# A language-model tower on one core: semaphores raised by TensorE, token numbers loaded in 8 KB runs, values formed ahead of scores

## The reference

```python
def tok(input_seq, emb_W, emb_b, Wq, bq, Wk, bk, Wv, bv, Wo, bo):
    emb = emb_W.T[input_seq] + emb_b
    q = (emb @ Wq.T + bq); k = (emb @ Wk.T + bk); v = (emb @ Wv.T + bv)   # 16 heads of 16
    probs = softmax(einsum('bqhd,bkhd->bhqk', q, k) / sqrt(d))
    y = einsum('bhqk,bkhd->bqhd', probs, v).reshape(b, s, e) @ Wo.T + bo + emb
    return layernorm over a sequence of y
h = tok(x, ...)
h = h + attn(layernorm(h), ...)
h = h + ffn(layernorm(h), ...)     # the 32 x 128 x 256 f32 result
```

## Time and profile before

| | us |
|---|---|
| median of 3 runs | 889.64 (888.16 to 892.07) |
| span of the profiled execution, first to last instruction | 888.7 |
| TensorE busy in the span | 710.7 |
| VectorE busy | 617.1 |
| GpSimd busy | 452.7 |
| ScalarE busy | 355.4 |

### The profile page before, as it was taken

One profiled execution on the slowest core, in us unless ns is written; L12 is line 12 of the kernel. 1 busy time (PEld: TensorE's weight loads), 2 busy tenths in 40 slices (PEclk: granted clock), 3 DMA queues, 4 the chain that ended last, 5 costly groups with the idle time before them and its releaser, 6 DMA issues. The chain is left out here.

```text
span 888.7 us, 20544 instructions
## 1 busy us (share of the span) xinstructions
PE 710.7 (80%) x7708; PEld 478.2 (54%) x7708; DVE 617.1 (69%) x913; ACT 355.4 (40%) x561; POOL 452.7 (51%) x257
## 2 busy tenths in 40 slices
PE   3576759886999999999999999976899689875744
PEld 3354534444677777777777777755676323322221
DVE  3599947888999999999999999963676501100005
ACT  2366635353445545445455544433555211010100
POOL 1588700002999999999999999981111000000000
PEclk9799869998999999999999999987999879979765
DMA  5100000000001010000000000005800679999936
GB/s 109 48 1 0 0 1 0 0 0 14 8 14 38 13 35 12 11 7 12 12 12 12 12 12 8 12 14 198 313 25 1 233 271 412 417 416 416 418 135 213
DMA packets 48891, 86.34 MB, mean 97 GB/s; under 512 B 5232, under 2 KB 32432, under 8 KB 48848
## 3 DMA queue, kind: packets, MB, share of 16 engines
q1 hardware_dynamic: 43248, 81.23, 25.1%
q10 hardware_dynamic: 5600, 4.53, 1.6%
HBM read 76.31 MB, written 9.44 MB: 96 GB/s over the span
## 5 line engine op out<-in xcount | busy, mean ns | idle before, releaser
L898 POOL TENSOR_TENSOR read<-state,q_pos 128x1024 f32<-128x1024 f32 x128 | 300.2, 2365 | 28.5 <-DVE state L1007 22.4
L1007 DVE TENSOR_TENSOR_SCAN state<-fac,ps_up 128x1024 f32<-128x1024 f32 x128 | 290.1, 2278 | 8.6 <-ACT fac L942 8.2
L942 ACT ACTIVATE fac<-ps_xf 128x1016 f32<-128x1016 f32 x128 | 130.2, 1018 | 176.1 <-PE ps_xf L1041 160.2
L1041 PE MATMUL ps_xf<-hot,xtab 64*128 64x128 f32 x2048 | 148.4, 284 | 11.0 <-ACT fac L942 8.9
L1041 PEld LDWEIGHTS ps_xf<-hot,xtab 64*128 64x128 f32 x2048 | 125.4, 188 | 58.0 <-ACT fac L942 43.4
L1041 PE MATMUL ps_up<-hot,utab 64*128 64x128 f32 x2048 | 140.0, 276 | 19.3 <-DVE state L1007 19.3
L1041 PEld LDWEIGHTS ps_up<-hot,utab 64*128 64x128 f32 x2048 | 126.4, 189 | 24.9 <-issue 17.6
L907 POOL TENSOR_TENSOR utab<-tab 128x1024 f32 (+1 forms) x32 | 64.7, 2022 | 94.4 <-SPq L85 94.4
L1086 PE MATMUL ps_o<-read,sel 128*32 128x256 f32 x1024 | 82.4, 393 | 4.0 <-POOL read L898 4.0
L1627 DVE COPY h_t<-ps_ht 128x512 f32<-128x512 f32 x16 | 10.3, 686 | 75.7 <-PE ps_ht L1655 75.7
L997 DVE TENSOR_TENSOR xtab<-tab,ps_k 128x1024 f32<-128x1024 f32 x64 | 59.5, 930 | 1.5 <-PE ps_k L1033 1.5
(11 more groups left out here) (202 smaller groups left out, 995.0 us busy)
## 6 DMA issues: line engine op xcount, KB each, us to landing
w_sb<-in_L_ffn_w SPq DMA_DIRECT2D x32, 2048.0 KB, 19.4
rec_out<-osb SPq DMA_DIRECT2D x128, 32.0 KB, 1.5
ao<-rec_out SPq DMA_DIRECT2D x8, 512.0 KB, 4.4
out_dram<-res ACTq DMA_DIRECT2D x8, 512.0 KB, 2.8
tok<-in_x SPq DMA_DIRECT2D x2, 512.0 KB, 11.2
exp_out<-eo SPq DMA_DIRECT2D x8, 128.0 KB
oq<-exp_out SPq DMA_DIRECT2D x2, 512.0 KB, 3.9
w_nat<-in_L_tok_Wq SPq DMA_DIRECT2D x1, 256.0 KB, 3.1
```

What stands on the lines that cost most here:

```text
L898: nc.gpsimd.tensor_tensor(read[n % 2][:], state[n % 4][:].rearrange("p (b i t) -> p b i t", b=2, i=IB), q_pos[x.s][:, :, x.k].unsqueeze(2) ...
L942: nc.scalar.activation(fac[n % 2][:].rearrange("p (n t) -> p n t", t=T)[:, :, 1:], ps_x[:].rearrange("p (n t) -> p n t", t=T)[:, :, 1:], A ...
L1007: nc.vector.tensor_tensor_scan(state[n % 4][:], fac[n % 2][:], ps_u[n % 2][:], 0.0, ALU.mult, ALU.add)\
L1041: last = nc.tensor.matmul(dst[:, b * 512 + col * T:b * 512 + (col + 1) * T], stationary[rows], pos[rows], start=True, stop=True)
```

## The change

The first block's semaphores are raised by TensorE, as the first thing in its program, and SP no longer does it. The token numbers become SP's first loads. They are paired b and b + 16, so each half of `tok` is one run of 2,048 numbers (8 KB) of x, which each of the 64 partitions gets whole. `emb_bc` and `bqk` move from ScalarE's queue to SP's, behind the token numbers, and Wv and Wo stay on SP behind those. Wq and Wk move to ScalarE's queue, behind `emb_w`. TensorE waits for the identity alone (`id_ok`) before its first transposes, and waits for `masks` just ahead of line 346. Wv is transposed together with Wq and Wk, ahead of q and k, and ScalarE copies it ahead of the logarithm. TensorE forms values and transposed embedding ahead of the scores. At the end of the kernel a quad now holds two sequences of the first half of the batch and two of the second, so its store becomes two DMAs of 256 KB, and `f_out` counts 32 per quad.

```diff
--- before.py
+++ after.py
@@ -192,32 +192,32 @@
         block = ctx.enter_context(nc.Block())
         ld_w = [sem(f"ld_w{n}") for n in range(4)]
         ld_e, ld_bq, ld_bv, ld_x = (sem(n) for n in ("ld_e", "ld_bq", "ld_bv", "ld_x"))
-        masks, w_tp, w_cp = sem("masks"), sem("w_tp"), sem("w_cp")
+        id_ok, masks, w_tp, w_cp = sem("id_ok"), sem("masks"), sem("w_tp"), sem("w_cp")
         emb_ok, q_mm, q_ok, k_ok = (sem(n) for n in ("emb_ok", "q_mm", "q_ok", "k_ok"))
         s_mm, e_tp, c_dg, c_mm, c1_ok, ln_ok = (sem(n) for n in ("s_mm", "e_tp", "c_dg", "c_mm", "c1_ok", "ln_ok"))
         vch = sem("v_chain0")
 
+        def weights(eng, n):
+            w = ("L0_tok_Wq", "L0_tok_Wk", "L0_tok_Wv", "L0_tok_Wo")[n]
+            eng.dma_start(w_nat[:, n], a[w].rearrange("(k p) i -> p k i", p=P)).then_inc(ld_w[n], 16)
+
         @block.sync
         def _(sp):
-            def weights(n):
-                w = ("L0_tok_Wq", "L0_tok_Wk", "L0_tok_Wv", "L0_tok_Wo")[n]
-                sp.dma_start(w_nat[:, n], a[w].rearrange("(k p) i -> p k i", p=P)).then_inc(ld_w[n], 16)
-
-            for n in range(2):
-                weights(n)
             for s in range(2):
-                src = a["x"].rearrange("(r s) t -> s r t", s=2)[s]
-                sp.dma_start(tok[s * C:(s + 1) * C], src.partition_broadcast(C)).then_inc(ld_x, 16)
+                src = a["x"].rearrange("(s r) t -> s (r t)", s=2)[s]
+                sp.dma_start(tok[s * C:(s + 1) * C].rearrange("p r t -> p (r t)"), src.partition_broadcast(C))\
+                    .then_inc(ld_x, 16)
+            sp.dma_start(emb_bc[:], a["L0_tok_emb_b"].rearrange("(k p) -> p k", p=P), allow_slow_non_contiguous=True).then_inc(ld_e, 16)
+            sp.dma_start(bqk[:, 0], a["L0_tok_bq"].rearrange("(k p) -> p k", p=P), allow_slow_non_contiguous=True).then_inc(ld_bq, 16)
+            sp.dma_start(bqk[:, 1], a["L0_tok_bk"].rearrange("(k p) -> p k", p=P), allow_slow_non_contiguous=True).then_inc(ld_bq, 16)
             for n in range(2, 4):
-                weights(n)
-            m["start"](sp)
+                weights(sp, n)
 
         @block.scalar
         def _(act):
             act.dma_start(emb_w[:], a["L0_tok_emb_W"].rearrange("(k p) c -> p k c", p=P)).then_inc(ld_e, 16)
-            act.dma_start(emb_bc[:], a["L0_tok_emb_b"].rearrange("(k p) -> p k", p=P), allow_slow_non_contiguous=True).then_inc(ld_e, 16)
-            act.dma_start(bqk[:, 0], a["L0_tok_bq"].rearrange("(k p) -> p k", p=P), allow_slow_non_contiguous=True).then_inc(ld_bq, 16)
-            act.dma_start(bqk[:, 1], a["L0_tok_bk"].rearrange("(k p) -> p k", p=P), allow_slow_non_contiguous=True).then_inc(ld_bq, 16)
+            for n in range(2):
+                weights(act, n)
             act.dma_start(bv_b[:], bcast_rows(a["L0_tok_bv"])).then_inc(ld_bv, 16)
             act.dma_start(bo_b[:], bcast_rows(a["L0_tok_bo"])).then_inc(ld_bv, 16)
             nc.scalar.preload_act_table(ACT.Ln)
@@ -226,12 +226,11 @@
                 act.wait_ge(w_tp, START + n + 1)
                 nc.scalar.copy(w_t[:, n], ps[n][:].rearrange("p (k o) -> p k o", k=KT)).then_inc(w_cp, 1)
 
-            for n in range(2):
+            for n in range(3):
                 copy_weights(n)
             act.wait_ge(c1_ok, START + 1)
             nc.scalar.activation(cnt1[:], cnt1[:], ACT.Ln).then_inc(ln_ok, 1)
-            for n in range(2, 4):
-                copy_weights(n)
+            copy_weights(3)
             act.wait_ge(ln_ok, START + 1)
             nc.scalar.preload_act_table(ACT.Exp)
 
@@ -248,8 +247,8 @@
             pch = Chain(pool, sem("p_chain0"))
 
             pch.link(nc.gpsimd.memset(ident[:], 0.0))
-            pch.link(nc.gpsimd.affine_select(out=ident[:], in_=ident[:], compare_op=ALU.not_equal, fill=1.0,
-                                             base=0, pattern=[[-1, P]], channel_multiplier=1))
+            nc.gpsimd.affine_select(out=ident[:], in_=ident[:], compare_op=ALU.not_equal, fill=1.0, base=0,
+                                    pattern=[[-1, P]], channel_multiplier=1).then_inc(id_ok, 1)
             for s in range(2):
                 pch.link(nc.gpsimd.iota(cid[s * C:(s + 1) * C], pattern=[[0, 1]], base=0, channel_multiplier=1,
                                         allow_small_or_imprecise_dtypes=True))
@@ -267,6 +266,7 @@
             pch.link(nc.gpsimd.memset(same_half[:], 0.0))
             for s in range(2):
                 pch.link(nc.gpsimd.memset(same_half[s * C:(s + 1) * C, s * C:(s + 1) * C], 1.0))
+            pool.wait_ge(id_ok, START + 1)
             nc.gpsimd.tensor_tensor(ident64[:], ident[:, 0:C], ident[:, C:P], ALU.add).then_inc(masks, 1)
             pch.link(nc.gpsimd.memset(m["sel"][:], 0.0))
             for q in range(4):
@@ -324,8 +324,9 @@
                                                    w_nat[:, n, ko, ki * P:(ki + 1) * P], ident[:])
                 last.then_inc(w_tp, 1)
 
-            pe.wait_ge(masks, START + 1)
-            for n in range(2):
+            m["start"](pe)
+            pe.wait_ge(id_ok, START + 1)
+            for n in range(3):
                 transpose_weights(n)
             pe.wait_ge(emb_ok, START + 1)
             pe.wait_ge(w_cp, START + 2)
@@ -339,24 +340,24 @@
                                             w_t[:, 1, ki, ko * P:(ko + 1) * P], emb_t[:, ki, 0:C],
                                             start=ki == 0, stop=ki == KT - 1)
             last.then_inc(q_mm, 1)
-            for n in range(2, 4):
-                transpose_weights(n)
+            transpose_weights(3)
             pe.wait_ge(c_dg, START + 1)
+            pe.wait_ge(masks, START + 1)
             for k in range(2):
                 nc.tensor.matmul(ps[6 + k][:], same_half[:],
                                  log_diag[:, k * PAIRS // 2:(k + 1) * PAIRS // 2].rearrange("p r c -> p (r c)"),
                                  start=True, stop=True).then_inc(c_mm, 1)
-            pe.wait_ge(q_ok, START + 1)
-            for k in range(KT):
-                pe.wait_ge(k_ok, START + k + 1)
-                nc.tensor.matmul(ps[k][:], q_t[:, k], k_heads[:, k].rearrange("p h c -> p (h c)"),
-                                 start=True, stop=True).then_inc(s_mm, 1)
             pe.wait_ge(w_cp, START + 3)
             for ki in range(KT):
                 nc.tensor.matmul(ps[5][:, 0:E], emb_t[:, ki], w_t[:, 2, ki], start=ki == 0, stop=ki == KT - 1)
             for k in range(KT):
                 last = nc.tensor.transpose(ps[5][:, E + k * P:E + (k + 1) * P], emb_t[:, k], ident[:])
             last.then_inc(e_tp, 1)
+            pe.wait_ge(q_ok, START + 1)
+            for k in range(KT):
+                pe.wait_ge(k_ok, START + k + 1)
+                nc.tensor.matmul(ps[k][:], q_t[:, k], k_heads[:, k].rearrange("p h c -> p (h c)"),
+                                 start=True, stop=True).then_inc(s_mm, 1)
 
 
     with ExitStack() as ctx:
@@ -1732,23 +1733,23 @@
             with nc.vector.Fori(0, TURNS) as i:
                 for s in range(2):
                     dve.wait_ge(f_mm[s], START + i + 1)
-                    dve.wait_ge(f_out[s], START + 16 * i)
+                    dve.wait_ge(f_out[s], START + 32 * i)
                     for j in range(QB):
-                        at = 2 * (j % 2) + j // 2
-                        last = nc.vector.tensor_tensor(res[s][:, at:at + 1], psx[s][j][:, 0:E].unsqueeze(1),
+                        last = nc.vector.tensor_tensor(res[s][:, j:j + 1], psx[s][j][:, 0:E].unsqueeze(1),
                                                        h2[:, bass.ds(2 * QB * i + QB * s + j, 1)], ALU.add)
                     last.then_inc(f_add[s], 1)
 
         @block.scalar
         def _(act):
-            dst = out.rearrange("(q j) t e -> q t j e", j=QB)
+            dst = out.rearrange("(z q p) t e -> z q t p e", z=2, p=2)
             with nc.scalar.Fori(0, TURNS) as i:
                 for s in range(2):
                     act.wait_ge(f_add[s], START + i + 1)
-                    act.dma_start(dst[bass.ds(2 * i + s, 1)].rearrange("q t j e -> (q t) j e"), res[s][:])\
-                        .then_inc(f_out[s], 16)
+                    for z in range(2):
+                        act.dma_start(dst[z, bass.ds(2 * i + s, 1)].rearrange("q t p e -> (q t) p e"),
+                                      res[s][:, 2 * z:2 * z + 2]).then_inc(f_out[s], 16)
             for s in range(2):
-                act.wait_ge(f_out[s], START + 16 * TURNS)
+                act.wait_ge(f_out[s], START + 32 * TURNS)
 
 
 # ---- launch: one core; inputs and outputs as the reference has them ----
```

## The result

| | before | changed | predicted |
|---|---|---|---|
| median of 5 runs, us | 889.35 (887.8 to 892.07) | 883.46 (881.69 to 884.7) | 881.9 (878.2 to 886.2) |
| ratio | | 0.9927, 95% interval 0.9908 to 0.9945 | 0.991 |
| span of the profiled execution, us | 888.7 | 880.2 | 881.0 |
| line 433 (now 434) begins, us | 29.69 | 23.18 | 21.7 |
| first store of the result to the end, us | 18.5 | 18.4 | 18.8 |

What follows compares the result with a forecast made beforehand. The first block was taken as bound by the token load, VectorE's counting, TensorE's last three steps and VectorE's tail. 8.0 us saved there less 0.3 for stores gave 7.7: 889.64 to 881.9 us, range 878.2 to 886.2.

Steps and rivals of the forecast that it cites:

- Semaphores: First block's start: TensorE raises all 22 in 1.5 us, through at 2.3 us, beside the loads.
- Token load: First block: 1.05 MB at 231 GB/s takes 4.5 us, landing at 7.1; `onehot` begins at 8.1 instead of 15.57.
- Weights: First block, two queues: Wv lands at 9.0, Wo's transposes end at 14.7, so line 346 begins then instead of 21.24.
- The clock: TensorE's line 346 runs partly at the upper clock level: 2.5 us, between 1.71 and 3.37.
- Values first: First block's end: values 1.25 us, then scores to ScalarE's last copy 2.50; block ends at 20.9 instead of 28.9.
- Stores: Result stores at the kernel's end, split in two: a cost of 0.3 us, at most 1.7, no gain.
- The sum: Whole kernel: 8.0 us from the first block less 0.3 for stores, 7.7 us, median 881.9.
- The loads are no faster: Rival on the token load: 8 KB runs no quicker than 512-byte ones; gain 2.2 us, 887.4; chance 0.08.
- The lower clock throughout: Rival: TensorE stays at the lower clock in the first block; gain 4.5 less 0.3, 885.4; chance 0.10.
- later block took the gain back: Rival: attention over classes meets a lower clock for longer, some 6 us, result within 0.5%; chance 0.03.
- the stores did not become the bound: Denies the rival that split stores bound the kernel, adding say 12 us, 894; chance 0.05.

Runs made afterwards that it cites:

- the run with the halves on two queues: The changed kernel with the second half of the token numbers as ScalarE's first load, the first half on SP; median 883.4 us, ratio 0.9924.
- the run with short runs first: The changed kernel with token numbers still first on SP's queue, but in the old 512-byte runs and one store per quad; median 886.55 us, ratio 0.9961.
- the small loads last: Token halves on two queues and bias on ScalarE's queue, with the two bqk loads moved behind Wv and Wo; median 884.9 us, ratio 0.9928.
- Long runs alone: The kernel before with only the new pairing: 8 KB token runs in the old queue place, stores in two; median 887.71 us, ratio 0.997.
- the run with the filled gap: The kernel before with 8 KB runs and stores in two, plus ten unused TensorE transposes behind Wo's; line 436 began at 27.32 us.

## Why the prediction was right

**Semaphores.** Right. They were priced at nothing. In the two runs on them TensorE's raising was worth 0.1 us with the old loads and -0.2 with the new ones.

**Token load.** The direction was right, and this is the term that was mis-sized. Forecast: 1 MB at 231 GB/s, there at 7.1. Measured: the second half at 9.9. The 231 GB/s itself was good (128 packets of 612 ns on 16 engines are 4.9 us). But I added it up as if Wq, Wk and the embedding beside it took no time from the same engines. From 2 to 8 us the rate was 88 to 370 GB/s for everything together, and the token packets ran from 2.2 to 9.2 us. In the run with the halves on two queues, where Wq and Wk stand behind a half, they ran from 2.2 to 7.2. `emb_bc`, forecast 0.2 us behind the tokens, came 0.9 us behind them. So `onehot` began at 11.54 instead of 8.1. The 5.62 us from there to `log_diag` were 5.61. Three readings of the prediction are off, and none moves its sum: the earlier trace rows have 115 to 259 GB/s from 7 to 15.5 us and not 117 to 179, the lower fixed part of a load is 1.5 us and not 1.4 (2.8 less 1.3), and the loads are 2.43 MB with the embedding.

The Trainium skill, page "SBUF — State Buffer", section on the DMA port swizzle, says that 64 partitions reach half of the ports. The run with one load to 128 partitions agrees: 320 against 612 ns, where that port map makes it a factor of two.

**Weights.** Mis-sized by the same step: Wv's transposes began at 12.46 instead of 9.0. q and k and Wo's transposes took 3.8 us (13.37 to 17.20) instead of 4.7, as the clock rose on the way at 16.4. Line 347 began at 17.20 instead of 14.7, 2.5 us late. That both paths arrive within 1 us of one another was right, though VectorE came last, by the 0.3 us that line 347's weight load waited, and not TensorE.

**The clock.** Line 347 to line 352 took 1.82 us (forecast 2.5, before 3.37), which gave 0.7 us back. The Trainium skill, page "TensorE: Matmul & The Clock Gate", section "What's actually happening", says that activity releases the throttled level. The trace agrees in the direction: with a wait of 0.5 us at most between Wo's transposes and line 347 (1.2 in the run with short runs first), nine of ten profiles with the new queues had it at 1.72 to 1.85 us. The tenth is the first execution with the small loads last, which had no wait at all. When the level rises is not fixed by the program (5.5 and 9.4 us after TensorE's first matmul in the two executions of one).

**Values first.** Right. Scores to ScalarE's last copy took 2.51 (forecast 2.50), and the order alone is 1.05 us by the run that undoes it.

**Stores.** 0.3 forecast, nothing measured (18.4 us from the first store to the end against 18.5), at the lower end of the forecast's bounds.

**The sum.** 2.5 us late at line 347, 0.7 back from the clock, 0.2 from values and scores, 0.2 between the two blocks (0.57 us instead of 0.79), 0.4 from the stores: 7.7 - 1.0 = 6.7, to rounding the 6.6 us by which the first block and the last stage got shorter. What each part of the change is worth does not add up. Long runs alone move line 346 by 3.7 us, the order of the queue with short runs by 2.8, both by 4.0. The rest, 2.5 us behind that line, is 1.05 of order and 1.4 of clock. That the span came within 0.8 us of the forecast is luck: the second block began 1.5 us later than forecast (23.18 against 21.7), and the stretch that nobody touched was 1.9 us shorter.

**The rivals.** "The loads are no faster" was half right: a long run is written no faster than partitions allow, and with short runs in the new place 5.2 of the 6.5 us remain. "The lower clock throughout" did not come in the changed kernel, but came for two lines in the run with long runs alone and took 1.4 us of its gain. In the program with the small loads last the late rise came and went, so there it is no cost of the program. Whether it would go in the run with long runs alone, too, is not shown: the run with the filled gap, its near twin, had it again. No later block took the gain back, and the stores did not become the bound.

**Better versions.** The halves on two queues with the bias on ScalarE's queue have the first block 1.7 us shorter than the changed kernel, but 0.9921 (0.9892 to 0.995) against 0.9927 can't be told apart. The 2.4 us of the half-rate load are open: one load that brings both halves to 128 partitions was not tried.

## What to carry to other kernels

The longest wait in a list is not the path: 8.4 us of TensorE's waiting were worth 0.1 us, as the token load ended later. Price a load by the partitions that it writes and by all that is in flight beside it, since rates read in a quiet stretch do not add up. Where several loads feed two paths that meet, moving one of them shifts the wait to the next: with `emb_t` 4.6 us sooner the block was 0.9 us shorter, and TensorE waited for weights.

## What the runs showed of the hardware

- A load of 8 KB runs to 64 partitions took 612 ns a packet by the median (446 to 634 in the other runs), one to 128 partitions 320 ns, with all partitions of a load reading one row in both.
- Two such halves issued at once from two queues were still served mostly one after the other, 4.9 and 7.5 us after issue.
- An issue can hold its engine: Wv's took 3.95 us behind 2,048 short runs and 0.59 behind 128 long ones.
- TensorE's clock rose 5.5 us after its first matmul in one execution and 9.4 in another of the same program, with no wait after that matmul in either. The granted-clock column shows 1.00 for the stretch before the first recorded change, where the durations of lines of one shape say the lower level. There the durations are to be read.
